# Row-score maxima taken from one or two banks per operation, and the turn of the maxima put eight scores later

## What is computed

```
q, k, v = split_heads(x @ Wq.T + bq), split_heads(x @ Wk.T + bk), split_heads(x @ Wv.T + bv)
q, k = rope(q), rope(k)
att = jnp.einsum('bhqd,bhkd->bhqk', q, k) / 4
att = softmax(where(tril, att, -inf), axis=-1)
y = einsum('bhqk,bhkd->bhqd', att, v) ... @ Wo.T + bo
x = layernorm(x + y)
x = layernorm(x + ffn(x))
```

## Time and profile before

| | |
|---|---|
| median of three runs | 2770.11 us |
| the profiled execution's own time | 2769.75 us |
| its span | 2767.9 us |
| TensorE matmuls busy | 2700.5 us, 98% of the span |
| VectorE busy | 1891.2 us, 68% |
| ScalarE busy | 1353.7 us, 49% |
| GpSimd busy | 95.3 us, 3% |
| mean granted TensorE clock | 0.988 of full speed |

### The profile page before, as it was taken

How to read it: one execution, slowest core, us unless ns; L and a number is a source line. 1 busy time by engine, 2 the same in 40 slices (tenths; PEclk the granted TensorE clock), 3 DMA queues, 4 the chain that set the end, 5 groups by cost and what they waited for, 6 DMA issues and landing times.

```text
span 2767.9 us, 38948 instructions
## 1 busy us (share of the span) xinstructions
PE 2700.5 (98%) x14816; PEld 1414.0 (51%) x14816; DVE 1891.2 (68%) x3938; ACT 1353.7 (49%) x2641; POOL 95.3 (3%) x174
## 2 busy tenths in 40 slices
PE   9799999999999999999999999999999999999998
PEld 5233333333333333333333332688888887888886
DVE  8899999888888888888887775533333362543343
ACT  5356666777766767777777777311111111001000
POOL 0000110001100011100000000000000000000000
PEclk9799999999999999999999999999999999999999
DMA  8721110011110011110001000411111132121100
GB/s 225 205 44 38 32 43 5 3 23 30 31 38 5 6 36 32 34 27 3 3 1 40 19 6 10 124 59 58 59 58 56 42 130 105 46 91 45 45 16 23
DMA packets 89050, 131.01 MB, mean 47 GB/s; under 512 B 26310, under 2 KB 63686, under 8 KB 85286
## 3 DMA queue, kind: packets, MB, share of 16 engines
q1 hardware_dynamic: 79068, 97.30, 11.3%
q0 software_dynamic: 6192, 22.23, 3.7%
q10 hardware_dynamic: 3616, 9.18, 1.2%
HBM read 82.46 MB, written 46.20 MB: 46 GB/s over the span
## 4 chain that ended last, share of the span: by engine, by line
PE 89%; DVE 6%; issue 2%; ACT 1%; DMA 1%; POOLq 0%; POOL 0%; ACTq 0%; DVEq 0%
PE wi_f L963 19%; PE at_o L506 18%; PE at_row L471 17%; PE at_key L485 16%; PE na_h L1181 13%; PE na_y L1193 3%; DVE at_segmax L557 3%; DVE fr_masked L553 1%; ACT at_probs L621 1%; PE at_key L488 1%; PE wi_p L808 1%; PE pr_main L125 1%; DMA pr_xt<-in_xT 1%; DVE pr_rest L219 0%; DVE pr_full L224 0%
## 5 line engine op out<-in xcount | busy, mean ns | idle before, releaser
L621 ACT ACTIVATE at_probs<-at_key 128x512 f32<-128x512 f32 (+3 forms) x2304 | 1127.1, 568 | 499.4 <-PE at_key L485 351.4
L557 DVE TENSOR_REDUCE at_segmax<-at_row 128x1 f32<-128x512 f32 x1792 | 1142.9, 684 | 167.1 <-PE at_row L471 163.0
L471 PE MATMUL at_row<-fr_k_stack,fr_q_stack 96*128 96x512 bf16 (+3 forms) x1152 | 403.7, 375 | 14.8 <-DVE at_segmax L553 10.5
L485 PE MATMUL at_key<-fr_q_stack,fr_k_stack 99*128 99x512 bf16 (+3 forms) x1152 | 414.1, 364 | 1.2 <-ACT at_probs L621 1.0
L471 PE MATMUL at_row<-at_k_stack,at_q_stack 96*128 96x512 bf16 (+3 forms) x1152 | 408.0, 364 | 1.8 <-DVE at_segmax L557 1.1
L485 PE MATMUL at_key<-at_q_stack,at_k_stack 99*128 99x512 bf16 (+3 forms) x1152 | 402.0, 364 | 7.7 <-ACT at_probs L621 7.1
L1181 PE MATMUL na_h<-fr_h,fr_h2w_h 128*128 128x512 f32 x1024 | 322.0, 396 | 1.4 <-DVE fr_h L704 1.4
L506 PE MATMUL at_o<-at_probs,fr_values 128*32 128x512 f32 (+3 forms) x2304 | 288.0, 572 | 0.0
L506 PE MATMUL at_o<-at_probs,at_values 128*32 128x512 f32 (+3 forms) x2304 | 286.9, 570 | 0.0
L553 DVE CUSTOM_DVE_ANT_0 fr_masked<-at_row,fr_causal 128x384 f32<-128x384 f32 (+3 forms) x512 | 244.0, 483 | 44.9 <-PE at_row L471 44.4
L471 PEld LDWEIGHTS at_row<-fr_k_stack,fr_q_stack 96*128 96x128 bf16 x1152 | 110.1, 98 | 310.7 <-DVE at_segmax L557 159.1
(11 more groups left out here) (120 smaller groups left out, 2466.3 us busy)
## 6 DMA issues: line engine op xcount, KB each, us to landing
hidden<-wi_h SPq DMA_DIRECT2D x64, 256.0 KB, 2.0
na_h2f<-hidden SPq DMA_DIRECT2D x8, 1024.0 KB, 7.5
q_parts<-pr_parts SPq DMA_DIRECT2D x16, 384.0 KB, 5.0
k_parts<-pr_parts SPq DMA_DIRECT2D x16, 384.0 KB, 6.8
at_q_stack<-q_parts POOLq DMA_DIRECT2D x48, 128.0 KB, 3.5
at_k_stack<-k_parts POOLq DMA_DIRECT2D x48, 128.0 KB, 3.8
outputs<-at_outs SPq DMA_DIRECT2D x128, 34.0 KB
pr_table<-in_table ACTq DMA_DIRECT2D x8, 512.0 KB, 7.6
```

What stands on the lines that cost most here:

```text
L471: last = nc.tensor.matmul(bank[:, 0:w], qst[u][0:SROWS, c, h, i * P:(i + 1) * P], kst[u][0:SROWS, h, s * CH:s * CH + w], start=True, stop= ...
L485: last = nc.tensor.matmul(bank[:, q0:CH], kst[u][0:SROWS + PARTS, h, j * P:(j + 1) * P], qst[u][0:SROWS + PARTS, c, h, q0:CH], start=True, ...
L557: nc.vector.tensor_reduce(segmax[:, n % 2, h * TPC + i, s:s + 1], row_ps[r % RING_R][:, 0:w], op=ALU.max, axis=AX.X).then_inc(rows_taken, 1)
L621: nc.scalar.activation(probs[:, g % RING_P, h, q0:CH], key_ps[m % RING_K][:, q0:CH], ACT.Exp, scale=HD ** -0.5).then_inc(probs_ready, 1)
```

## The change

In blocks 0 to 4 (`PAIRED` = 5) two neighbouring row units of the same i and h, whose banks lie next to each other in the ring, are taken by one VectorE operation. The four banks become slices of one PSUM tensor. If neither of the two is diagonal, one reduction over 2 x 512 columns writes two columns of `segmax`. If the second is diagonal, one custom operation runs over 512 + (i + 1) x 128 columns, with a causal mask of double width, and writes one column only; the other column is left as it was, so `segmax` is set to the masking value at the start of each of these five blocks (`clear`), and the first operation of the block waits for that. The operation waits until both banks are ready and hands both back when it has ended. TensorE's row, key and values matmuls stay as they are. The constant `causal` becomes twice as wide, 512 KB in place of 256 KB in the first DMAs of the program, and moves to another place of SBUF, as does `masked`.

A unit in the last bank of the ring can't begin a pair. Over the five blocks there are 240 row units; the rule gives 75 pairs (50 of two full banks, 25 with a diagonal) and leaves 90 single. By block, from 0 to 4: 0, 10, 15, 18 and 32 pairs.

`TURN_LAG` goes from 4 to 8 in all blocks, so each turn but the last stands four row units later in both queues.

The diff:

```diff
--- before.py
+++ after.py
@@ -44,7 +44,8 @@
 TERMS = [(0, 0), (0, 1), (1, 0), (1, 1), (0, 2), (2, 0)]
 SROWS = HD * len(TERMS)
 TURN = -1
-TURN_LAG = 4
+TURN_LAG = 8
+PAIRED = 5
 SLACK = 28 * CH
 FIRST_EARLY = 3
 FIRST_AHEAD = 4
@@ -285,6 +286,18 @@
     return blocks, rows, groups
 
 
+def row_pairs(blocks, rows):
+
+    firsts, r = set(), 0
+    while r + 1 < len(rows):
+        n, i, h, s = rows[r]
+        if i != TURN and n < PAIRED and rows[r + 1] == (n, i, h, s + 1) and r % RING_R != RING_R - 1:
+            firsts.add(r)
+            r += 1
+        r += 1
+    return firsts
+
+
 def row_width(c, i, s):
     return CH if s < c else (i + 1) * P
 
@@ -332,6 +345,11 @@
     out_after = {min(g + 1, NG - 1): n for n, g in last_group.items()}
     diagonal_at = [r for r, (n, i, _, s) in enumerate(rows) if i != TURN and s == blocks[n][1]]
     diagonal = {r: k for k, r in enumerate(diagonal_at)}
+    first_row = {}
+    for r, (n, i, _, _) in enumerate(rows):
+        if i != TURN:
+            first_row.setdefault(n, r)
+    paired = row_pairs(blocks, rows)
     MR = PARTS * QUAD * TPC
     PREP_QUAD = NQUAD - 1
     prep_block = blocks.index((PREP_QUAD, NCH - 1))
@@ -358,7 +376,8 @@
         maxrest = sb("maxrest", [P, QUAD * TPC])
         maxparts = sb("maxparts", [P, 2, PARTS, QUAD * TPC], BF16)
         maxrows = sb("maxrows", [MR, 2, P], BF16)
-        row_ps = [ctx.enter_context(nc.psum_tensor(f"at_row{i}", [P, CH], F32)) for i in range(RING_R)]
+        row_all = ctx.enter_context(nc.psum_tensor("at_row", [P, RING_R * CH], F32))
+        row_ps = [row_all[:, i * CH:(i + 1) * CH] for i in range(RING_R)]
         key_ps = [ctx.enter_context(nc.psum_tensor(f"at_key{i}", [P, CH], F32)) for i in range(RING_K)]
         o_ps = ctx.enter_context(nc.psum_tensor("at_o", [P, CH], F32))
 
@@ -370,6 +389,7 @@
         values_loaded = [sem(f"values_loaded{q}") for q in range(NQUAD)]
         rows_ready = sem("rows_ready")
         rows_taken = sem("rows_taken")
+        cleared = sem("cleared")
         split = sem("split")
         maxparts_ready = sem("maxparts_ready")
         max_spilled = sem("max_spilled")
@@ -545,17 +565,28 @@
             def segment(r):
 
                 n, i, h, s = rows[r]
-                w = row_width(blocks[n][1], i, s)
-                dve.wait_ge(rows_ready, r + 1)
-                if s == blocks[n][1]:
-                    if diagonal[r] >= 2:
-                        dve.wait_ge(rows_taken, diagonal_at[diagonal[r] - 2] + 1)
-                    nc.vector.tensor_tensor_reduce(out=masked[:, diagonal[r] % 2, 0:w], in0=row_ps[r % RING_R][:, 0:w], in1=causal[:, CH - w:CH],
+                c = blocks[n][1]
+                count = 2 if r in paired else 1
+                end = s + count - 1
+                w = (count - 1) * CH + row_width(c, i, end)
+                at = (r % RING_R) * CH
+                dve.wait_ge(rows_ready, r + count)
+                if end == c:
+                    k = diagonal[r + count - 1]
+                    if k >= 2:
+                        dve.wait_ge(rows_taken, diagonal_at[k - 2] + 1)
+                    nc.vector.tensor_tensor_reduce(out=masked[:, k % 2, 0:w], in0=row_all[:, at:at + w], in1=causal[:, 2 * CH - w:2 * CH],
                                                    scale=1.0, scalar=MASKED, op0=ALU.add, op1=ALU.max,
-                                                   accum_out=segmax[:, n % 2, h * TPC + i, s:s + 1]).then_inc(rows_taken, 1)
+                                                   accum_out=segmax[:, n % 2, h * TPC + i, end:end + 1]).then_inc(rows_taken, count)
                     return
-                nc.vector.tensor_reduce(segmax[:, n % 2, h * TPC + i, s:s + 1], row_ps[r % RING_R][:, 0:w],
-                                        op=ALU.max, axis=AX.X).then_inc(rows_taken, 1)
+                nc.vector.tensor_reduce(segmax[:, n % 2, h * TPC + i, s:end + 1],
+                                        row_all[:, at:at + w].rearrange("p (b t) -> p b t", b=count),
+                                        op=ALU.max, axis=AX.X).then_inc(rows_taken, count)
+
+            def clear(n):
+
+                nc.vector.memset(segmax[:, n % 2, :, :], MASKED).then_inc(cleared, 1)
+                dve.wait_ge(cleared, n + 1)
 
             def finish(n):
 
@@ -586,9 +617,11 @@
             for r, (n, i, _, _) in enumerate(rows):
                 if i == TURN:
                     take_turn(r)
-                else:
+                elif r - 1 not in paired:
+                    if r == first_row[n] and n < PAIRED:
+                        clear(n)
                     segment(r)
-                    if r == last_row[n]:
+                    if r + (r in paired) == last_row[n]:
                         finish(n)
                         if n == NB - 2:
                             prep.invert_den(dve, 0)
@@ -664,8 +697,8 @@
 
         at = 2 * STACK + VALUES
         self.x1t = [place(f"x1t{u}", at + u * X1T, [P, 2, DH, CH], F32R) for u in range(2)]
-        self.masked = place("masked", at + X1T, [P, 2, CH])
-        self.causal = place("causal", at + X1T + 2 * CH, [P, CH])
+        self.masked = place("masked", at + X1T, [P, 2, 2 * CH])
+        self.causal = place("causal", at, [P, 2 * CH])
         self.h2f = [place("h2f_a", at, [P, FK // 2, CH]), place("h2f_b", 2 * STACK, [P, FK // 2, CH])]
         at += 2 * X1T
         self.ident32 = place("ident32", at, [P, P])
@@ -1299,7 +1332,7 @@
     "x": [T, D], "xT": [NCH, P, DH, CH], "table": [NCH, P, 2, CH],
     "WqT": [D, D], "WkT": [D, D], "WvT": [D, D], "WoT": [D, D],
     "bias": [P, 2 * DH], "bv": [P, DH], "bo": [D],
-    "ident": [P, P], "mask": [P, P], "causal": [P, CH], "ones": [PARTS, QUAD * T // 2],
+    "ident": [P, P], "mask": [P, P], "causal": [P, 2 * CH], "ones": [PARTS, QUAD * T // 2],
     "w1T": [D, F], "w2T": [D, F], "h1T": [F, F], "h2T": [F, F], "w3T": [F, D],
     "s1": [P, FK], "s2": [P, FK], "hs1": [P, FK], "hs2": [P, FK], "s3": [D],
 }
@@ -1336,7 +1369,7 @@
         ones=np.full((PARTS, QUAD * T // 2), one, np.float32),
         ident=np.eye(P, dtype=np.float32),
 
-        causal=np.where(np.arange(CH)[None, :] - (CH - P) > p[:, None], MASKED, 0.0).astype(np.float32),
+        causal=np.where(np.arange(2 * CH)[None, :] - (2 * CH - P) > p[:, None], MASKED, 0.0).astype(np.float32),
         mask=np.where(p[:, None] > p[None, :], MASKED, 0.0).astype(np.float32),
     )
```

## The result

The changed kernel takes 2786.09 us (median of four runs, 2784.72 to 2788.11) against 2769.13 us for the kernel before in the same comparison: a ratio of 1.0063, 95% interval 1.0048 to 1.0078. It is slower by 17 us. The forecast was slower by 7.7, up to 2784 in the range: the sign was right, the size was less than half of what came. The profiled execution is 2786.86 us with a span of 2785.0.

A forecast was written before the change was run, and what follows sets the result against it. TensorE was taken as the bound, held back by VectorE up to about 226 us. Terms -0.6 + 1.3 + 4.0 + 3.9 + 0.3 = +8.9 us on 2769.75, less 1 for kinder groups, gave 2777.5 us, range 2765 to 2784.

The forecast's parts named there:

- up to the copy of block 0: Row units before the first key and block 0's keys: VectorE never waits; pairs save 1.3, clears cost 0.7: -0.6 us.
- keys of block 1: Stage of block 1's keys: 0.45 us of new VectorE idle in five groups, less 15 pairs' saving: +1.3 us.
- keys of block 2: Stage of block 2's keys: 8.5 groups blocked by 0.65 us, less 1.5 us of waits already there: +4.0 us.
- keys of block 3: Stage of block 3's keys: seven of nine groups blocked by 0.55 us each, TensorE without slack: +3.9 us.
- The saving per pair: VectorE's queue in the paired blocks: each pair drops 0.067 us once, at most 5.0 us for 75 pairs.
- `clear`: Five MEMSETs at the start of blocks 0 to 4: 0.22 us each, between 0.1 and 0.35, 1.1 us together.
- The wider constant: `causal` in the program's first DMAs, another 256 KB: 0, at most +1 us if table loads are pushed back.
- The turn: Four units later: -1.2 us in two turns, +1.5 behind `finish`, together +0.3; later blocks 0, between -2 and +1.
- The saving arrives: Rival one, chance 0.19: the pairs' saving arrives and the ring loses nothing, -5.1 us, 2764.7 us.
- gain and loss cancel: Rival two, chance 0.19: ring terms of +8.2 become about +3.5, against -0.6 and later turns: 2769 to 2772 us.
- The pair is no shorter than two: Rival four, chance 0.05: two banks in one operation cost more, 7.5 us on VectorE per tenth of a us: 2781 us.
- The clock falls more often: Rival three, chance 0.05: TensorE's clock falls at every fourth of 29 groups, seven more falls, +12.6 us, 2790 us.

The follow-up runs named there:

- single operations and the ring in pairs: Kernel before with TURN_LAG 8, old single operations, but the same 75 pairs' banks waited for and handed back together: 2785.92 us, ratio 1.0066.
- lag 8: Kernel before with TURN_LAG = 8 in place of 4 and nothing else: 2765.08 us, ratio 0.9986.
- five banks: Changed kernel with five row banks, two key banks, 87 pairs: 2932.32 us; its control with single units and TURN_LAG 8: 2923.78 us.
- half of the pairing: Kernel before, TURN_LAG 8, single operations: waiting for both banks but handing back singly, 2772.15 us; taking singly but handing back together, 2771.52 us.
- lag 12: Kernel before with TURN_LAG = 12 in place of 4: 2761.63 us, ratio 0.9964.

## Why the prediction fell short, by its own steps

The mechanism was named rightly: four banks become two double ones, and the waits of the ring decide. The time came out above the range because of the sizes. By stage, without what the later start of the stage (0.5 us) adds; the forecast's +0.3 for the first turns and its -1 for kinder groups stand in no row:

| stage | forecast us | measured us |
|---|---|---|
| up to the copy of block 0 | -0.6 | +6.9 |
| keys of block 1 | +1.3 | +3.5 |
| keys of block 2 | +4.0 | +5.1 |
| keys of block 3 | +3.9 | +4.3 |
| later blocks | 0 (-2 to +1) | -3 |

- **The step that failed** is the first: "Ahead of that (the row units before the first key and the keys of block 0) VectorE never waits, and its gain is real". VectorE didn't wait with four single banks. I carried that over to the ring of pairs, and charged the ring only from block 1's keys on: -0.6 us was put where +6.9 came, 7.5 of the 9 us that the forecast was short. With single operations and the ring in pairs c0 comes 6.4 us after that of lag 8 alone, with the changed kernel 7.0. In sight was that TensorE ran at 1.2 GHz up to 140 us and later (granted clock 0.50 from 130 to 140 us before). At that level a row unit takes 0.40 from start to start and a key unit with its mask 0.53, so two row units and a key unit between take 1.3 us, longer than the 1.14 in which a pair is emptied; my group was computed at the upper level, and no stage was computed at the lower. Not in sight was that the pairs would also make the clock rise later: the first values of block 0 take 1.87 us after, 1.00 before (147.30 to 148.30).
- **Keys of block 1** were under-sized by 2.2 us, and by some 3 if the 0.95 is left out that the lag alone gains in this stage. I counted 0.45 of new idle in five groups, 2.25 in all. VectorE stands idle for 6.2 us here, against 1.5 with lag 8: 4.7 of new idle. The largest hole lies behind block 2's `finish`, where TensorE's clock had fallen and a pair had to be completed behind values of 1.87 us; with lag 8 it is 1.00:

```profile
176.52 1.22 DVE L582 TENSOR_REDUCE at_segmax<-at_row 128x2 f32<-128x1024 f32 x1 [3.13 <-PE at_row L491]
```

- **Keys of blocks 2 and 3** held within 1.1 us. The single group was nearly right: from values to values it lasted 3.06 us without and 3.79 with a blocked unit, 0.73 more where 0.63 was forecast. TensorE's timeline after:

```profile
262.88 1.07 PE L526 MATMUL at_o<-at_probs,fr_values 128*32 128x512 f32 x8
...
265.69 0.39 PE L491 MATMUL at_row<-fr_k_stack,fr_q_stack 96*128 96x512 bf16 x1 [0.55 <-DVE at_segmax L578]
...
266.67 1.06 PE L526 MATMUL at_o<-at_probs,fr_values 128*32 128x512 f32 x8
...
269.73 1.06 PE L526 MATMUL at_o<-at_probs,fr_values 128*32 128x512 f32 x8
```

- **The saving per pair** was right (0.06 at 138.93 us, 0.05 over 14 pairs with five banks). The 0.533 us for 512 columns, which no row of before gives, is 0.539 by the recorded lengths after (683 to 1222 ns). The Trainium skill's figure in "VectorE: DVE Perf Modes", section "The TRN2 errata — SBUF-src ops pay a fixed extra latency per instruction", would give an estimated 0.125 per operation dropped; no distance between starts here shows that much. But the saving wasn't collected: VectorE's queue got shorter only to stand idle longer.
- **`clear`** put 0.31 to 0.35 us between the start of `finish` and the first operation of the next block (1.25 and 1.29 against 0.94 before), 0.22 forecast, near the upper end of 0.35. **The wider constant**: the stage began 0.5 us later, within what it scatters between kernels (115.8 to 120.2 us).
- **The turn**: -1.05 from the lag alone at c3, -1.2 forecast; but all of it comes at the first of the two turns (1.06 at c1), where 0.60 at each was forecast, and the changed kernel had none of it at c3. The sum is near by luck. In the later blocks I took 0; the turns there had waited 8.7 us together, which the profile of before showed had I grouped them by line over the whole stage. The run with the lag alone gained about 3 there, and so did the changed kernel.
- **Rivals.** *The saving arrives* and *gain and loss cancel* are false. *The pair is no shorter than two* is false by its row. *The clock falls more often*: no fall at every fourth group was seen; from 160 to 230 us the granted clock is 1.00 but for 0.83 at 170 and at 220, two falls as in the earlier trace rows. What came was a later rise at the start of the stage, which I hadn't among the rivals; some 1.3 us of the loss are put down to it above. The rival's time (2790) was near, its mechanism wasn't.
- **The signs.** VectorE idle before row units between 210 and 260 us: 9.8 us (over 8 expected), 2.7 before. TensorE's waits for VectorE from 190 to 260 us: 10.1 us, 2.1 before. These held. The copy of block 3 came 20.3 us later, not 7 to 9.
- **The sum** is off by a little in itself: 2769.75 + 8.9 - 1 is 2777.65, and the keys of block 2 were counted with 0.65 a group where the working gives 0.63.

The Trainium skill, "Perfetto Trace Analysis", section "Matmuls", has the rule that independent groups rotate through banks so that emptying one overlaps the next. The runs agree and give its size in this kernel at c3: 20.9 us with two double banks, 5.4 with a fifth bank, 5 with half of the pairing.

## What to carry to other kernels

Merging two operations on a ring halves the number of slots unless the ring grows with it: the saving per operation (here 0.06 us) must be set against one more slot of waiting on both sides, and in each stage at the clock that this stage has, not at the best one. Test such a change first by its waits and hand-backs alone, with the old operations; here that single run gave the answer. A small instruction that needs a slot behind a serial step (the turn) belongs further behind it in an in-order queue, as far as its consumer allows: here 8 or 12 places gained over 4, and 15 no more.

## What was unexpected of the hardware

- An operation over two PSUM banks costs nothing for the boundary between them. The mean recorded lengths of the masked maximum after are 416, 548 and 684 ns for 256, 384 and 512 columns in one bank, and 819, 956 and 1089 for 640, 768 and 896 in two: 132 to 137 ns for each 128 columns, also from 512 to 640. A reduction over 1024 columns (1222 ns) takes 0.06 us less from start to start than two of 512.
- After the same kind of wait the clock fell in one execution and not in another. With lag 8, then with lag 12, TensorE behind block 2's `finish`:

```profile
164.78 0.39 PE L471 MATMUL at_row<-fr_k_stack,fr_q_stack 96*128 96x512 bf16 x1 [1.44 <-DVE at_segmax L557]
...
165.31 1.83 PE L506 MATMUL at_o<-at_probs,fr_values 128*32 128x512 f32 x8
```
```profile
162.64 0.39 PE L471 MATMUL at_row<-fr_k_stack,fr_q_stack 96*128 96x512 bf16 x1 [1.45 <-DVE at_segmax L557]
...
163.18 1.06 PE L506 MATMUL at_o<-at_probs,fr_values 128*32 128x512 f32 x8
```

  The waits are 1.44 and 1.45 us, the values behind them take 1.83 (1.2 GHz) and 1.06 (2.4 GHz). So a fall after a wait was not certain, and a kernel's median can hold both.
